# Attention and gated layer on one core: one score-maximum piece a group fewer, and more of them ahead of the first group

## What is computed

```python
xn = _layernorm(x, axis=-1)
s = _L0_attn_ref(xn, w_qkv, b_qkv, w_out, b_out)      # softmax(q k / 4 + alibi, causal) v, then w_out
g = _silu(_L0_ffn_ref(xn, w_gate, w_up, w_down))      # silu(gate) * up, then down, hidden 1360
x = x + s * g
```

## Time and profile before

| what | us |
|---|---|
| median of 3 runs | 840.68 |
| lowest and highest | 839.41 and 840.71 |
| the profiled execution | 836.7 |
| its span on the core | 834.9 |

### The profile page before, as it was taken

How to read it: one execution, slowest core, us unless ns; L and a number is a source line. 1 busy time by engine, 2 the same in 40 slices (tenths; PEclk the granted TensorE clock), 3 DMA queues, 4 the chain that set the end, 5 groups by cost and what they waited for, 6 DMA issues and landing times.

```text
span 834.9 us, 16148 instructions
## 1 busy us (share of the span) xinstructions
PE 796.8 (95%) x5926; PEld 350.6 (42%) x5926; DVE 631.0 (76%) x1774; ACT 472.5 (57%) x631; POOL 132.6 (16%) x183
## 2 busy tenths in 40 slices
PE   5999999999999999999899999999999999999998
PEld 3444544444444444444343343343433344343333
DVE  6656877743533565664799999999999999996546
ACT  5434285333132232222488888888888788887540
POOL 4223132223032131131000000000000003530000
PEclk9999999999999999999899999999999999999999
DMA  7474322348202201101121122222125233653635
GB/s 264 131 214 165 137 91 77 113 124 299 104 1 76 76 1 38 63 1 41 62 63 60 58 72 80 80 67 79 55 66 166 81 91 107 198 144 116 215 138 219
DMA packets 71056, 88.40 MB, mean 106 GB/s; under 512 B 26926, under 2 KB 37166, under 8 KB 70464
## 3 DMA queue, kind: packets, MB, share of 16 engines
q1 hardware_dynamic: 70848, 87.10, 32.2%
q0 software_dynamic: 128, 0.27, 0.2%
HBM read 51.15 MB, written 35.93 MB: 104 GB/s over the span
## 4 chain that ended last, share of the span: by engine, by line
PE 70%; DVE 16%; DMA 5%; issue 4%; ACT 3%; POOL 1%; SPq 0%; DVEq 0%; ACTq 0%
PE psum L1537 12%; PE psum L1494 9%; PE psum L1560 9%; PE psum L1561 9%; DVE mx L1207 8%; PE psum L1571 5%; PE psum L1572 5%; PE psum L1512 4%; DVE mshown L1203 3%; PE psum L1388 2%; PE psum L1390 2%; PE psum L1389 2%; DMA q_scr<-qk_stage 2%; PE psum L1521 2%; PE psum L1596 1%
## 5 line engine op out<-in xcount | busy, mean ns | idle before, releaser
L922 ACT ACTIVATE probs<-psum,exp_scale 128x1024 f32<-128x1024 f32 (+1 forms) x320 | 310.3, 1028 | 71.3 <-PE psum L1521 51.1
L1203 DVE CUSTOM_DVE_ANT_0 mshown<-psum,ahead 128x384 bf16<-128x384 f32 (+3 forms) x512 | 220.3, 487 | 2.8 <-PE psum L1494 0.4
L1494 PE MATMUL psum<-QKs 51*128 51x512 f16 (+3 forms) x768 | 186.2, 333 | 16.0 <-DVE mx L1207 6.3
L1537 PE MATMUL psum<-probs,Vs 128*32 128x512 f32 (+3 forms) x1536 | 162.3, 511 | 0.2 <-ACT probs L922 0.2
L1207 DVE TENSOR_REDUCE mx<-psum 128x1 f32<-128x512 f32 x256 | 157.6, 681 | 3.3 <-PE psum L1494 2.4
L1512 PE MATMUL psum<-QKs 53*128 53x512 f16 (+3 forms) x768 | 139.0, 331 | 1.6 <-ACT probs L922 1.4
L1560 PE MATMUL psum<-X,room 128*128 128x512 f16 (+1 forms) x352 | 133.6, 379 | 0.0
L1561 PE MATMUL psum<-X,room 128*128 128x512 f16 (+1 forms) x352 | 133.4, 379 | 0.0
L1494 PEld LDWEIGHTS psum<-QKs 51*128 51x128 f16 x768 | 52.1, 93 | 152.0 <-DVE mx L1203 78.9
L954 ACT ACTIVATE room<-psum,gate_half 128x512 f32<-128x512 f32 (+1 forms) x44 | 30.2, 687 | 101.2 <-PE psum L1561 101.2
L800 POOL TENSOR_TENSOR room<-room 128x512 f16<-128x512 f32 (+1 forms) x44 | 50.9, 1156 | 172.2 <-ACT room L959 172.2
(11 more groups left out here) (162 smaller groups left out, 922.1 us busy)
## 6 DMA issues: line engine op xcount, KB each, us to landing
o_scr<-osum SPq DMA_DIRECT2D x32, 256.0 KB, 3.2
QKs<-q_scr SPq DMA_DIRECT2D x96, 64.0 KB
QKs<-k_scr SPq DMA_DIRECT2D x96, 64.0 KB
q_scr<-qk_stage SPq DMA_DIRECT2D x16, 256.0 KB, 2.4
k_scr<-qk_stage SPq DMA_DIRECT2D x16, 256.0 KB, 2.2
v_scr<-v_stage SPq DMA_DIRECT2D x16, 256.0 KB, 2.1
Vs<-v_scr SPq DMA_DIRECT2D x16, 256.0 KB
probs<-in_L_attn_x SPq DMA_DIRECT2D x4, 1024.0 KB, 11.6
```

The lines of the kernel that those rows point to most:

```text
L922: nc.scalar.activation(probs[n % PSLOTS][:, 2 * pair:2 * pair + 2, 0:COLS[n]], s_bank[pair][:, :, 0:COLS[n]], ACT.Exp, scale=exp_scale[:, ...
L1203: last = nc.vector.tensor_tensor_reduce(out=mshown[tiles_read(at) % 2][:, cols], in0=m_bank[bank][:, cols], in1=ahead[:, CH - keys:], scal ...
L1494: last = nc.tensor.matmul(tile[:, hh, :], Qs[s][rows, pair + hh, qb * P:(qb + 1) * P], Ks[s][rows, pair + hh, k0:k0 + keys], start=(hh == ...
L1537: last = nc.tensor.matmul(pv_bank[32 * h:32 * h + 32, CH - cols:CH], Vs[s][:, kb, h::QH], probs[n % PSLOTS][:, h, at:at + cols], start=(kb ...
```

## The change

`GROUP` loses one M, out of the only run of four; the other letters stand as before. Since a group now holds 41 pieces and there are 42 a group to be done, the lead over the scores is no longer constant: the new list `AHEAD` makes it 25 pieces at group 0's start and one less with each group, down to 11. `line(t)` gives the running number of the first piece that group t's stretch takes, `early` takes all before `line(0)`, and `divmod` turns running numbers into pieces.

```diff
-GROUP = "MPMMPSMMSMPMMSSMMMSSMMPMSMMSPMMSMPMM" \
-        "SMSMMPMSMMMMSSMPMMSPMMSSMMPMMSMSMMSM"
+GROUP = "MPMMPSMMSMPMMSSMMMSSMMPMSMMSPMMSMPM" \
+        "MSMSMMPMSMMMSSMPMMSPMMSSMMPMMSMSMMSM"
+AHEAD = [LEAD + (QUADS - 2 - t) * (NITEM - GROUP.count("M")) for t in range(QUADS - 1)]
+
+
+def line(t):
+
+    return (t + 1) * NITEM + AHEAD[t] if t < QUADS - 1 else QUADS * NITEM
 def group_order(t):
-    items = [(t + 1, i) for i in range(LEAD, NITEM)] + [(t + 2, i) for i in range(LEAD)]
+    items = [divmod(i, NITEM) for i in range(line(t), line(t + 1))] if t < QUADS - 1 else []
+    if t == QUADS - 2:
+        items.append((QUADS, ROWS_AT))
...
-        else:
+        elif items:
             out.append(("maximum", *items.pop(0)))
-    return [w for w in out if w[1] >= 0 and (w[0] != "maximum" or w[1] < QUADS or w[1:] == (QUADS, ROWS_AT))]
+    return [w for w in out if w[1] >= 0]
...
-    early = [(0, i) for i in range(NITEM) if i != ROWS_AT] + [(1, i) for i in range(LEAD)]
+    early = [divmod(i, NITEM) for i in range(line(0)) if i != ROWS_AT]
```

## The result

| what | before | after |
|---|---|---|
| median of the runs | 840.04 | 883.29 |
| lowest and highest | 838.57 and 840.71 | 880.86 and 885.35 |
| profiled execution, its span | 836.7, 834.9 | 884.92, 883.1 |

What follows compares the result with a forecast made beforehand. PE was taken to bound the gated stage, VectorE the attention groups. Losses 2.3 + 9.45 + 1.65 + 4.95 = 18.35 less 5.25 gained gave +13.1 us: 853.8 us against 840.68, range 846 to 861.

Steps and rivals of the forecast that it cites:

- (a): Attention groups: 11 wide reads leave VectorE's stretch, 6.75 us less, minus 1.5 for the shift; gain 5.25 us, between 3 and 6.75.
- the attention groups give nothing: Rival: shifted pieces starve VectorE by as much as one read a group; 859.1 us, chance 0.05.
- (b): Gated stage: 11 more fills on PE at 0.207 us each, +2.3 us.
- (c): Gated stage: four pieces in a row behind three down-projection tiles stall PE 3.15 us each, +9.45 us.
- (d): Gated stage: four pieces in a row behind two odd tiles stall PE 0.82 us each, +1.65 us.
- Faster: Rival: runs of four behind down tiles cost nothing, VectorE reading before the tile's three steps; 837.9 us, chance 0.05.
- (e): Gated stage: PE's clock falls to half after each of three long stalls, 1.65 us each, +4.95 us, between 0 and 10.
- falls for long: Rival: longer clock falls, 858.9 us, or also behind short stalls, 857.1; run of seven may prolong group 0's; chance 0.12.
- (f): Attention groups: loads of a slot's keys and values still arrive in time; 0 us, 1 if PE were 3 us early.
- The rows of maxima ... cost nothing: Rows of maxima, POOL's three small steps and SP's transfer come earlier than the scores needing them; no cost.

Runs made afterwards that it cites:

- e3_aligned41: The kernel before with one wide piece of the maxima left out of every group, its M taken from the run of four, nothing shifted; 841.02 us.
- e1_cap3: The changed kernel with at most three pieces in a row behind a tile of the gated stage, the rest at its end; 865.18 us, ratio 1.0302.
- e8_scores_first: The kernel before with group 0's first two scores moved up behind the second piece after the gated stage; ratio 0.9989.
- e2_shift14: The kernel before, 42 pieces a group, with a constant lead of 25 pieces instead of 11, at most three in a row in the gated stage; 870.92 us.
- e5_cap_rows_late: e1_cap3 with the last entry for the rows of maxima put back behind the scores it had been moved ahead of; 860.96 us, ratio 1.0256.
- e9_thin_fills: The kernel before with every fill of the maxima on PE cut to 64 columns a block, VectorE reading full width; 832.79 us.

## Why the prediction was right and wrong, by its own steps

**(a), the step that failed.** It said that a steady group gains one read, 23.92 to 23.31, because "PE's work there is at most 23.12, and less by the fill that leaves, so PE doesn't take over by its sum". The sentence is true of sums, and sums over a whole group don't set its length; what did was which pieces stood beside which of PE's work. An aligned group with one read less gained 0.12 (`e3_aligned41`). It said further that the shift costs "0.5 us in all", at most 3. It costs 1.2 to 1.8 us in each of eleven groups, against 23.79. Group 0, where the sum has 1.0 us of loss, lost 3.0, with 3.4 us more at half a clock. The rival "the attention groups give nothing" was set aside because VectorE's slack of three banks "is larger than the shift of any one stretch". That was never worked out. The last interval alone gets 1.02 us more of reads (4.30 for 3.28), and it follows one that is full as well, so PE comes to it with no lead to spend. The table by intervals could have been written before any run, from the pieces' widths, the string and the trace of before. PE's own row wasn't known then, but the measured intervals bound it from above: the longer of these and of the new reads, summed, is 25.9 for group 5, on the right side of 23.91 and 0.3 from the 25.59 measured. Taken gain 5.25; measured, from the gated stage's end to the end of the kernel, a loss of 27.5.

**(b)** 2.3 us for eleven fills, 0.207 each: `e1_cap3` has 2.5 for twelve, 0.21 each. Right.

**(c) and (d)** 9.45 and 1.65: the three long stalls are 3.23, 2.98 and 3.23 us, the two short ones 0.78 and 0.96. Together 11.18, forecast 11.10. Places, causes and sizes are right, and the rival "Faster", by which VectorE would read ahead of the tile's steps, is out.

**(e)** The mechanism was right and the size off: 4.95 forecast for three falls, two came, each of the short kind: 3.3 us x half for one and 3.4 x half for the other, 3.35 together. The prediction took the Trainium skill's account of micro-idles ("TensorE: Matmul & The Clock Gate", section "A second HAM failure mode: psum-queue depth-cycling") to bring the clock down behind (d) too. The windows from 298.20 and 371.00 show it at 1.00, so that rival is out here; the section gives no size of the idles, so the two don't contradict it. What did come of the rival "falls for long" is its last sentence: behind the run of seven the half clock lasted 10.1 us and not 6.7. With six in a row (`e1_cap3`) it lasted 6.7, but 10.1 also in `e8_scores_first`, so the run's length isn't shown to be the cause.

**(f)** 0, at most 1: one wait of 0.5 us on the values' load over thirteen groups. Right for this change, and near its edge: at a lead that stays at 25 the same load cost PE 3.8 us (`e2_shift14`), and with short reads 9.2, one wait being 5.47.

**"The rows of maxima ... cost nothing"** was wrong for the last of them. It asked what comes early enough, and not what is queued behind that entry on SP. That was the denominators' load, and some 2 us by `e5_cap_rows_late`.

The costs in the gated stage, priced row by row, came out within about 1 us (18.35 forecast, 17.3 measured), with (e) 1.6 too high. What failed was the gain, which was priced from means.

## What to carry to other kernels

Where two engines hand work over through few buffers and each keeps to a fixed order, a first estimate of the time is the sum, over the intervals between the fixed points of that order, of the longer of the two engines' work. Here it came within 0.3 us of 24 to 26 for three leads, 0.7 low for a fourth and up to 1.1 low for single groups; that is rough, but the sums over a whole group missed the loss altogether. Before moving work in such an order, write both rows interval by interval for the new alignment; a removed piece gains only in an interval that its engine sets, and a shift costs wherever a heavy piece meets a light one. When an entry moves, read on every engine's queue what it has been moved ahead of.

## What the runs showed of the hardware

**PE's busy time holds waiting.** The same instructions of a group are busy for 23.12 us in the earlier trace rows and for 21.65 with short reads, at the same clock of 1.00. A busy time of 23.12 in 23.92 looked like an engine close behind the other; it was in part the other engine's pace. The Trainium skill says that matmul busy time is a poor measure of how near a kernel is to its roofline ("Perfetto Trace Analysis", section "Identifying the Most-Contended Engine"), and the two windows agree. The reason that the Trainium skill gives there is that matmuls are pipelined; that the busy time takes in waiting for another engine is what these windows add.

**The clock isn't told by the length of a stall.** Idle stretches of 3.23, 2.98 and 3.23 us in a full stream were followed by a held clock, a fall of 3.3 us and one of 3.4. After 3.16 us and a sparse start of group 0, PE was at half a clock for 10.1 us, and for 6.7 in the kernel before, after 3.17; after 2.61 us, in `e8_scores_first`, for 10.1. In `e9_thin_fills`, waits of 0.40, 0.40 and 0.32 us between thin fills came just ahead of a clock of 0.73, here in group 2:

```profile
458.28 0.20 PE L1494 MATMUL psum<-QKs 51*128 51x64 f16 x1 [0.40 <-DVE mx L1207]
458.87 0.20 PE L1494 MATMUL psum<-QKs 51*128 51x64 f16 x1 [0.40 <-DVE mx L1207]
460.07 0.20 PE L1494 MATMUL psum<-QKs 51*128 51x64 f16 x1 [0.32 <-DVE mx L1207]
```

The windows around them:

```profile
452.97:459.00 6.03, 5.09 (x69) 2.53 (x70) 6.03 (x15) 4.85 (x7) 0.00 (x0) 1.00 0.50 128
459.00:462.00 3.00, 2.68 (x27) 0.82 (x23) 2.81 (x5) 2.17 (x3) 0.00 (x0) 0.73 0.59 162
```

A fall came in groups 1 to 7, 10, 13 and 14. With PE so light a group still got longer by it, 23.97 against 23.12 us at a held clock. The Trainium skill ("TensorE: Matmul & The Clock Gate", section "A second HAM failure mode: psum-queue depth-cycling") describes a kernel that idles briefly as it cycles through PSUM banks while its clock goes up and down; this trace agrees with it. Whether the waits or the thinner fills brought the clock down was not separated.
